# Two 16-head attention stages: scores from 32-row by 64-column pieces, four PSUM banks shared with the P transposes, multiplication by halves

## What is computed

```python
# self attention: 16 heads of 8 channels
qkv = layernorm(x) @ Wqkv.T + b                      # q, k, v: heads of D = 8
scores = einsum('bhsd,bhtd->bhst', q, k) / sqrt(8)
scores = scores * exp(-abs(dd) * abs(s - t))         # a decay with the distance
x = x + (softmax(scores) @ v) @ out_w.T + out_b
# cross attention: 16 query heads, 4 key heads repeated four times
q = (layernorm(x) @ Wq.T + bq) / sqrt(8); k, v from the context
sim = where(causal & (mask != 0), q @ k.T, lowest)
x = x + layernorm(softmax(sim) @ v) @ Wo.T + bo
```

## Time and profile before

| what | value |
|---|---|
| median of three runs | 2212.42 us (2212.34 to 2218.19) |
| the profiled execution | 2209.22 us |
| its span | 2207.2 us |
| mean granted TensorE clock | 0.936 of full |
| stage sa, first to last multiplication | 32.4 to 336.1 us |
| stage ca, first to last masking | 368.7 to 644.8 us |
| busy over the span | PE 84%, DVE 71%, ACT 51%, POOL 60% |

### The profile page before, as it was taken

How to read it: one execution, slowest core, us unless ns; L and a number is a source line. 1 busy time by engine, 2 the same in 40 slices (tenths; PEclk the granted TensorE clock), 3 DMA queues, 4 the chain that set the end, 5 groups by cost and what they waited for, 6 DMA issues and landing times. The chain is left out here.

```text
span 2207.2 us, 63464 instructions
## 1 busy us (share of the span) xinstructions
PE 1858.3 (84%) x24029; PEld 1389.7 (63%) x24029; DVE 1557.0 (71%) x3269; ACT 1125.3 (51%) x2119; POOL 1316.0 (60%) x1041
## 2 busy tenths in 40 slices
PE   5999997999984542899999999999999569837776
PEld 3777775777764232466666666666666559626665
DVE  6888885777779652687777777777776777674444
ACT  3677774777753350354454554545544442334444
POOL 3676764777763024576676777766766236207887
PEclk9999997999999766899999999999999879969999
DMA  8000000000003204000000000000000141322221
GB/s 231 15 1 0 0 0 14 17 16 14 15 5 96 76 16 85 15 2 2 1 0 0 0 0 0 0 0 0 0 0 1 48 134 48 98 65 62 66 66 51
DMA packets 102034, 69.66 MB, mean 32 GB/s; under 512 B 12222, under 2 KB 95296, under 8 KB 101552
## 3 DMA queue, kind: packets, MB, share of 16 engines
q1 hardware_dynamic: 89840, 51.72, 8.2%
q0 software_dynamic: 8496, 15.61, 2.8%
q10 hardware_dynamic: 3600, 1.01, 0.2%
HBM read 45.24 MB, written 23.53 MB: 31 GB/s over the span
## 5 line engine op out<-in xcount | busy, mean ns | idle before, releaser
L1260 POOL TENSOR_TENSOR wa_rot<-wa_rot,wa_cross 128x1024 f32<-128x1024 f32 x128 | 302.4, 2362 | 161.7 <-DVE wa_cross L1452 161.7
L1449 DVE TENSOR_TENSOR wa_rot<-wa_ps_qk,cos 128x1024 f32<-128x1024 f32 x128 | 156.1, 1219 | 97.8 <-PE wa_ps_qk L1303 97.5
L1265 POOL TENSOR_TENSOR wa_sd<-wa_sd,wa_mx 128x1024 f32<-128x1024 f32 x64 | 121.7, 1902 | 110.2 <-DVE wa_mx L1469 110.2
L1422 ACT COPY wa_pt<-wa_ps_t 128x1024 f32<-128x1024 f32 x64 | 64.8, 1012 | 235.5 <-PE wa_ps_t L1346 235.5
L324 POOL TENSOR_TENSOR sa_sd<-sa_sd,sa_mx 128x1024 f32<-128x1024 f32 x64 | 121.7, 1902 | 94.0 <-DVE sa_mx L504 93.9
L1323 PEld LDWEIGHTS wa_ps_t<-ident,wa_rot 128*128 128x128 f32 x1024 | 114.7, 141 | 87.1 <-issue 84.1
L324 POOL TENSOR_TENSOR ca_sd<-ca_sd,ca_mx 128x1024 f32<-128x1024 f32 x64 | 121.7, 1902 | 72.5 <-DVE ca_mx L504 72.5
L1323 PE MATMUL wa_ps_t<-ident,wa_rot 128*128 128x128 f32 x1024 | 136.4, 276 | 1.5 <-ACT wa_qt L1400 1.5
L1370 PE MATMUL wa_ps_o<-l_wo,wa_ot 128*128 128x128 f32 x1024 | 127.6, 279 | 8.1 <-ACT wa_ot L1428 8.1
L1303 PE MATMUL wa_ps_qk<-l_wq,wa_xt 128*128 128x512 f32 x256 | 128.5, 625 | 2.2 <-ACT wa_xt L1394 0.4
L1303 PE MATMUL wa_ps_qk<-l_wk,wa_xt 128*128 128x512 f32 x256 | 128.1, 623 | 2.4 <-DVE wa_cross L1452 2.4
(11 more groups left out here) (307 smaller groups left out, 5224.8 us busy)
## 6 DMA issues: line engine op xcount, KB each, us to landing
x_res<-in_x_dram SPq DMA_DIRECT2D x16, 256.0 KB, 7.1
ca_ctx_t<-in_ctx_t_dram SPq DMA_DIRECT2D x64, 64.0 KB, 1.8
x_dram<-xp_row SPq DMA_DIRECT2D x16, 256.0 KB, 2.3
xn_dram<-r_xn SPq DMA_DIRECT2D x16, 256.0 KB, 2.3
x_res<-x_dram SPq DMA_DIRECT2D x16, 256.0 KB, 5.3
cs_ctx_t<-in_ctx_t_dram SPq DMA_DIRECT2D x16, 256.0 KB, 2.8
l_ffn<-in_f_w_dram SPq DMA_DIRECT2D x2, 2048.0 KB, 11.5
cm_ctx<-in_ctx_dram SPq DMA_DIRECT2D x16, 256.0 KB, 2.9
```

What stands on the lines that cost most here:

```text
L1260: pool.tensor_tensor(rot[n][:], rot[n][:], cross[n][:], ALU.add).then_inc(rotated[n], 1)
L1265: pool.tensor_tensor(sd[:, v], sd[:, v], mx[:, v].unsqueeze(2).to_broadcast([P, H1, SEQ]), ALU.subtract).then_inc(sub_ready, 1)
L1449: dve.tensor_tensor(rot[n][:].rearrange("p h s d -> p (h s) d"), src.rearrange("p h s d -> p (h s) d"), bc(k.cos[:], 1, 2 * H1), ALU.mult)
```

## The change

The pieces of the scores contract 32 rows (one group of four heads), with a q that isn't masked: `qm`, `pair_mask` and the doubled q are gone, and `split_groups` becomes `q_copy` over 128 columns. The pieces are still 8 per tile, now at 4 row positions x 2 column positions of the array, and each group of heads has a PSUM bank of its own (`ps_st`, 4 banks, of which the scores take 256 columns each). The transposed P uses the first two of the same four banks. So `scores` waits also for an earlier `p_copy`, and `p_transpose` of tile t waits until the multiplication has read the first two banks of tile t + 2 (`half_taken`). The multiplication is cut in two halves of 512 columns in sa, against a decay copied four times beforehand, and in four quarters of 256 columns in ca, with the count raised after the second. All parts but ScalarE's `normalise` have one more step of lag, the orders within the steps change, and LAST is 7.

```diff
--- before.py
+++ after.py
@@ -251,7 +251,8 @@
         xn = sb("xn", [P, 2, P])
         xt = sb("xt", [P, 2, P])
         k_sb = sb("k", [P, 2, P])
-        qm = sb("qm", [P, 2, 2, P])
+        q_sb = sb("q", [P, 2, P])
+        decay_all = None if cross else sb("decay_all", [P, GRP, SEQ])
         km = sb("km", [P, 2, GRP, P])
         vbd = sb("vbd", [P, SLOTS, 2, PAIRS, 2, D0 + 1])
         sd = sb("sd", [P, 4, H0, SEQ])
@@ -267,10 +268,11 @@
 
         ps_xq = ps("ps_xq", [P, 4, P])
         ps_kv = ps("ps_kv", [P, 4, P])
-        ps_s = ps("ps_s", [P, H0, SEQ])
-        ps_pt = ps("ps_pt", [P, PAIRS, P])
+        ps_st = ps("ps_st", [P, 4, 512])
         ps_o = ps("ps_o", [P, 512])
         ps_y = ps("ps_y", [P, 512])
+        s_ps = ps_st[:, :, 0:GRP * SEQ]
+        pt_ps = ps_st[:, 0:2].rearrange("p b (n t) -> p (b n) t", t=P)
         o_ps = ps_o[:, 0:H0 * (D0 + 1)].rearrange("p (h d) -> p h d", d=D0 + 1)
         ot_ps, y_ps = ps_y[:, 0:P], ps_y[:, P:2 * P]
 
@@ -283,14 +285,14 @@
         q_made, q_ready = sem("q_made"), sem("q_ready")
         kv_made, k_ready, v_ready, km_ready = sem("kv_made"), sem("k_ready"), sem("v_ready"), sem("km_ready")
         s_made, s_taken, mx_ready = sem("s_made"), sem("s_taken"), sem("mx_ready")
-        scores_begun = sem("scores_begun")
+        half_taken, decay_ready = sem("half_taken"), sem("decay_ready")
         sub_ready, p_ready = sem("sub_ready"), sem("p_ready")
         pt_made, pt_ready = sem("pt_made"), sem("pt_ready")
         o_made, rec_ready, o_ready = sem("o_made"), sem("rec_ready"), sem("o_ready")
         ot_made, ot_ready, y_made = sem("ot_made"), sem("ot_ready"), sem("y_made")
         xb_ready, x_added, o_kept, summed = sem("xb_ready"), sem("x_added"), sem("o_kept"), sem("summed")
 
-        LAST = 6
+        LAST = 7
 
         nc.scalar.preload_act_table(ACT.Exp)
         block = c.enter_context(nc.Block())
@@ -342,7 +344,7 @@
                     pool.tensor_tensor(xb[:, v % 2], k.x_res[:, t], k.a_bo[:], ALU.add).then_inc(xb_ready, 1)
 
             def step(i, u):
-                for stage, behind in ((split_heads, 1), (add_bias, 6), (subtract_max, 2)):
+                for stage, behind in ((split_heads, 2), (add_bias, 7), (subtract_max, 3)):
                     if has(i - behind, NT):
                         stage(i - behind, (u - behind) % SLOTS)
 
@@ -377,25 +379,27 @@
             def scores(t, v):
                 pe.wait_ge(q_ready, t + 1)
                 pe.wait_ge(km_ready, t + 1)
+                if late(t, 3):
+                    pe.wait_ge(pt_ready, t - 2)
                 if late(t, 1):
                     pe.wait_ge(s_taken, t)
-                pe.sem_inc(scores_begun, 1)
-                for odd in range(2):
-                    for pair in range(2):
-                        g, of = 2 * pair + odd, slice(pair * SEQ, (pair + 1) * SEQ)
-                        for b in range(2):
-                            rows = slice(b * SEQ, (b + 1) * SEQ)
-                            mm = pe.matmul(ps_s[rows, GRP * g:GRP * g + GRP], qm[of, v % 2, odd, rows],
-                                           km[of, v % 2, :, rows], start=True, stop=True)
+                for g in range(H0 // GRP):
+                    of = slice(g * GRP * D0, (g + 1) * GRP * D0)
+                    for b in range(2):
+                        rows = slice(b * SEQ, (b + 1) * SEQ)
+                        mm = pe.matmul(s_ps[rows, g], q_sb[of, v % 2, rows], km[of, v % 2, :, rows],
+                                       start=True, stop=True)
                 mm.then_inc(s_made, 1)
 
             def p_transpose(t, v):
                 pe.wait_ge(p_ready, t + 1)
-                if late(t, 1):
+                if has(t + 2, NT):
+                    pe.wait_ge(half_taken, t + 3)
+                else:
                     pe.wait_ge(pt_ready, t)
                 flat = sd[:, v % 4].rearrange("p (n h) s -> p n (h s)", h=2)
                 for n in range(PAIRS):
-                    mm = pe.transpose(ps_pt[:, n], flat[:, n], k.ident[:])
+                    mm = pe.transpose(pt_ps[:, n], flat[:, n], k.ident[:])
                 mm.then_inc(pt_made, 1)
 
             def values(t, v):
@@ -421,8 +425,8 @@
                 pe.matmul(y_ps, ot_sb[:, v % 2], k.a_wo[:], start=True, stop=True).then_inc(y_made, 1)
 
             def step(i, u):
-                for stage, behind in ((scores, 2), (o_transpose, 6), (p_transpose, 4), (x_transpose, 0), (values, 5),
-                                      (out_project, 6), (project, 0)):
+                for stage, behind in ((scores, 3), (o_transpose, 7), (x_transpose, 1), (p_transpose, 5), (out_project, 7),
+                                      (values, 6), (project, 1)):
                     if cross and stage in (o_transpose, out_project):
                         continue
                     if has(i - behind, NT):
@@ -464,7 +468,7 @@
                 act.wait_ge(pt_made, t + 1)
                 if late(t, 2):
                     act.wait_ge(o_made, t - 1)
-                act.copy(pt[:, v % 2], ps_pt[:]).then_inc(pt_ready, 1)
+                act.copy(pt[:, v % 2], pt_ps).then_inc(pt_ready, 1)
 
             def o_copy(t, v):
                 act.wait_ge(ot_made, t + 1)
@@ -474,8 +478,8 @@
                 act.activation(ot_sb[:, v % 2], ot_ps, ACT.Identity, bias=bv[:]).then_inc(ot_ready, 1)
 
             def step(i, u):
-                for stage, behind in ((kv_copy, 1), (normalise, 0), (o_copy, 6), (x_copy, 0), (p_copy, 4),
-                                      (exponential, 3)):
+                for stage, behind in ((kv_copy, 2), (o_copy, 7), (x_copy, 1), (exponential, 4), (p_copy, 5),
+                                      (normalise, 0)):
                     if cross and stage is o_copy:
                         continue
                     if has(i - behind, NT):
@@ -496,20 +500,27 @@
                 if late(t, 4):
                     dve.wait_ge(pt_made, t - 3)
                 if cross:
-                    dve.scalar_tensor_tensor(out=sd[:, v % 4], in0=bc(k.mask_all[:, t], 1, H0), scalar=NEG, in1=ps_s[:],
-                                             op0=ALU.mult, op1=ALU.add).then_inc(s_taken, 1)
+                    for g in range(H0 // GRP):
+                        masked = dve.scalar_tensor_tensor(out=sd[:, v % 4, GRP * g:GRP * (g + 1)],
+                                                          in0=bc(k.mask_all[:, t], 1, GRP), scalar=NEG,
+                                                          in1=s_ps[:, g].rearrange("p (h s) -> p h s", s=SEQ),
+                                                          op0=ALU.mult, op1=ALU.add)
+                        if g == 1:
+                            masked.then_inc(half_taken, 1)
+                    masked.then_inc(s_taken, 1)
                 else:
-                    dve.tensor_tensor(sd[:, v % 4], ps_s[:], bc(k.decay[:], 1, H0), ALU.mult).then_inc(s_taken, 1)
+                    by_group = sd[:, v % 4].rearrange("p (g h) s -> p g (h s)", h=GRP)
+                    decays = bc(decay_all[:].rearrange("p h s -> p (h s)"), 1, 2)
+                    dve.tensor_tensor(by_group[:, 0:2], s_ps[:, 0:2], decays, ALU.mult).then_inc(half_taken, 1)
+                    dve.tensor_tensor(by_group[:, 2:4], s_ps[:, 2:4], decays, ALU.mult).then_inc(s_taken, 1)
                 dve.wait_ge(s_taken, t + 1)
                 dve.tensor_reduce(mx[:, v % 4], sd[:, v % 4], AX.X, ALU.max).then_inc(mx_ready, 1)
 
-            def split_groups(t, v):
+            def q_copy(t, v):
                 dve.wait_ge(q_made, t + 1)
                 if late(t, 2):
                     dve.wait_ge(s_made, t - 1)
-                dve.scalar_tensor_tensor(out=qm[:, v % 2], in0=bc(ps_xq[:, 1], 1, 2), scalar=bq[:],
-                                         in1=k.pair_mask[:].to_broadcast([P, 2, P]), op0=ALU.add, op1=ALU.mult)\
-                   .then_inc(q_ready, 1)
+                dve.tensor_scalar(q_sb[:, v % 2], ps_xq[:, 1], bq[:], None, ALU.add).then_inc(q_ready, 1)
 
             def divide(t, v):
                 dve.wait_ge(o_made, t + 1)
@@ -541,10 +552,14 @@
                 dve.scalar_tensor_tensor(out=k.mask_all[:, bass.ds(t - 3, 4)], in0=k.mask_in[:, bass.ds(t - 3, 4)],
                                          scalar=0.0, in1=bc(k.future[:], 1, 4), op0=ALU.is_equal, op1=ALU.max)
 
+            if not cross:
+                dve.tensor_scalar(decay_all[:], bc(k.decay[:], 1, GRP), 1.0, None, ALU.mult).then_inc(decay_ready, 1)
+                dve.wait_ge(decay_ready, 1)
+
             rest = LoadedStats(dve, k, rest_st, (rest_sums, rest_ready, rest_newton), 1, 16)
 
             def step(i, u):
-                for stage, behind in ((softmax, 2), (divide, 5), (split_groups, 0), (residual, 6), (sums, 6)):
+                for stage, behind in ((softmax, 3), (residual, 7), (divide, 6), (sums, 7), (q_copy, 1)):
                     if has(i - behind, NT):
```

(2 more changed lines are left out.)

## The result

The changed kernel took 2279.9 us (median of four runs, 2273.8 to 2288.18) against 2214.91 us for the kernel before (four runs, 2212.34 to 2218.19): 1.0295 times the time, with a 95% interval of 1.0256 to 1.0334. It is slower, by about 65 us. The profiled execution took 2273.8 us, with a span of 2272.0; before it was 2209.22 and 2207.2.

What follows compares the result with a forecast made beforehand. TensorE's own row of parts was taken as the bound in sa and ca. 63 x 0.30 + 63 x 0.60 - 5 = 52 us on the profiled 2209.2 gave 2261 (2264 on the median's footing); range 2242 to 2298.

Steps and rivals of the forecast that it cites:

- What bounds the kernel: In stages sa and ca, TensorE's own row of parts sets the pace and no semaphore stops it; steps 4.76 and 4.43 us.
- Scores, 1.03 to 0.62: TensorE's scores stretch per tile: two waves of eight pieces instead of four waves of four, 1.03 us becoming 0.62.
- Rival 1: Scores pieces still run four together, so nothing pays for the wait: 52 us more, 2316; chance 0.11, whole or part.
- The wait, +0.71 and +1.01: Ahead of `p_transpose`, TensorE stands while DVE multiplies the first half: +0.71 us per tile in sa, +1.01 in ca.
- E + 0.93: Forecast start of `p_transpose` in sa, 0.93 us after E, the moment the next load after the scores could start.
- +0.30 and +0.60 per tile: Net step growth in sa and ca, wait less the 0.41 us scores saving, giving steps of 5.06 and 5.03 us.
- "-5 in all" at the heads: At stage heads the low clock makes saved waves worth 0.42 each, and first and last tiles skip the wait: -5 us.
- The rest, "all at nothing": Copy of transposed P, POOL, decay copy, constant load and lags cost nothing; without cover a few tenths of a us, once.
- Rival 2: At the head of `p_transpose` TensorE doesn't stand, so only the saving of 0.41 a tile stays: faster, 2161; chance 0.07.
- Rival 3: TensorE's clock falls from its new pauses in sa and ca: +50 us, 2314, for a tenth of both stages; chance 0.04.
- The "+50": Cost in us if the clock fell for a tenth of the two stages, doubling TensorE's some 4 us for 13 tiles.

## Why the prediction was right

The forecast was 2261 us for a profiled execution, 52 over the kernel before; it measured 2273.8, 64.6 over.

- **What bounds the kernel** held: TensorE's row of parts set the pace. The kernel with neither wait nor new pieces showed that the rest of the change moves nothing.
- **Scores, 1.03 to 0.62**: exact on TensorE. Rival 1 is out: sixteen loads in 0.23 us and 0.62 to the next part. In the step they bring 0.37 and 0.36, not 0.41. The table of the Trainium skill (TensorE: Matmul & The Clock Gate, "Measured speedup vs the span model"), in which four 32-row positions gain 3.07 times and not 4, would by the prediction's estimate have added 0.13 a tile. These 32-row pieces show no such loss: 0.62 was forecast without it and measured.
- **The wait, +0.71 and +1.01**: measured alone, +0.73 and +1.01. The start of `p_transpose` was put at E + 0.93 and came at 206.04 - 205.06 = 0.98: DVE's start 0.17 (0.18 in most steps), the half 0.69, the release 0.12. Each was 0.01 to 0.04 over the row it was taken from. In ca it was put at 1.12 and came at 543.70 - 542.54 = 1.16.
- **+0.30 and +0.60 per tile** became 5.12 - 4.76 = +0.36 and 5.08 - 4.43 = +0.65. This is the mis-sized term of the sum: 0.05 to 0.06 in each of 126 tiles, some 7 us. Most of it is DVE's start after the scores, taken from rows of the wide pieces (0.14 and 0.26), which with the new pieces is 0.18 and 0.30. By the stages' lengths, with their heads and ends, it was +0.38 (23.8 / 63) and +0.59 (37.4 / 63), which is 61 us against the 57 of 63 x 0.90.
- **"-5 in all" at the heads** was not there. The first row maximum of sa did come earlier, at 31.9 instead of 33.7 us. But the first 13 tiles then took 72.0 us instead of 66.7, +0.41 each, no less than in the cruise. What the waves saved at the low clock was lost again; which part of that is the wait and which the clock was not tried by itself.
- **The rest, "all at nothing"** held, except 5 us in untouched stages, which vary by more on their own. So 57 + 4 + 5 - 2 against my 57 - 5, which is the 13 us between +65 and +52. That the copy cost nothing held for this order of the parts alone.
- **Rival 2** was one edit away. The place named for it, the head of `p_transpose`, was right: with `values` in the shadow the sign turns, to a ratio of 0.9884, 0.9800 with the copy split and 0.9772 with the wait by quarters too. The price named, 0.41 a tile, was reached in the cruises of the fastest version: its steps vary, but their means of 4.32 and 4.05 are 4.76 and 4.43 less 0.44 and 0.38. Over the whole stages it is less, 303.7 - 281.4 = 22.3 and 276.1 - 253.9 = 22.2 us, or 0.35 a tile.
- **Rival 3** was undervalued. It did not happen, at pauses of 0.79 and 1.02 us a step. But with the third quarter waited for, the loads stood for 1.24 to 1.47 us in each step of ca, and the clock fell for much of the stage. The Trainium skill (TensorE: Matmul & The Clock Gate, "Why this matters for your kernels") warns of gaps between bursts of matmuls much longer than these. So it can't be read as a promise that shorter ones are safe: in ca 1.02 us a step left the granted clock at 1.00, and pauses 0.2 to 0.5 us longer didn't. The "+50" for a fall in a tenth of the stages was low too: in that run the clock fell, came back twice and then stayed down for the last 310 of the 454 us of ca. The stage took 454.3 - 313.5 = 141 us more, of which the longer wait itself is 63 x 0.33 = 21.

## What to carry over

- When two producers on one engine are made to share banks, the engine waits for the consumer between them. Price that as a chain of measured links (consumer's start, its piece, its release) less what already lies in its shadow, and then look for independent work to put into the shadow: here moving one part turned +3% into -1%.
- A filled pause uncovers the next loop through the same banks, here the copy; split it at the same boundary as the first.
- A pause in a loop has a price beyond its length. Here 0.33 us more of waiting per step, worth 21 us, made the stage 141 us longer, since the clock fell.

## What the runs showed of the hardware

- Sixteen 32x64 pieces of 256 columns take 0.62 us to the next part, as two waves of eight that start 0.27 apart, where sixteen 64x64 pieces took 1.03 in four waves, the first two 0.26 apart: no loss from running eight positions at once. But DVE, which waits for them, starts 0.04 later after that moment than with the wide ones.
- Splitting a DVE operation is cheap: 1024 elements took 1.22 us, two halves 0.61 + 0.68 = 1.29, four quarters 1.41.
- A longer wait, the only edit, brought the granted clock down. With the loads standing for 1.24 to 1.47 us in steps of 5.29 to 5.41 it fell in mid-stage; at 1.02 us in steps of 5.08 it was 1.00 from 393 us to the end of the stage. But in sa of the kernel with the whole wait, steps of 5.72 held as well (granted clock 1.00 from 200 to 250 us), with pauses as long (1.38). What decides between these was not settled.
